# LSTM by cells: the first exact sweep becomes a second preparing sweep with short-fraction matmuls on 124 cells

## The reference

```python
x_proj = jnp.einsum('btd,gd->btg', x, W_ih) + b_ih + b_hh
def step(carry, xp):
    h, c = carry
    gates = xp + h @ W_hh.T
    i, f, g, o = jnp.split(gates, 4, axis=-1)
    c = jax.nn.sigmoid(f) * c + jax.nn.sigmoid(i) * jnp.tanh(g)
    h = jax.nn.sigmoid(o) * jnp.tanh(c)
    return ((h, c), h)
_, hs = jax.lax.scan(step, (h0, c0), jnp.swapaxes(x_proj, 0, 1))
```

## Time and profile before

| | us |
|---|---|
| median of the runs | 2495.29 |
| the profiled execution | 2494.4 |
| its span, first to last instruction | 2492.6 |
| busy TensorE matmul / weight load | 2193.6 / 1884.3 |
| busy VectorE / ScalarE / GpSimd | 1716.5 / 1504.2 / 156.2 |
| the three exact sweeps with their tests | 1664.4 to 2359.0 |

### The profile page before, as it was taken

One profiled execution on the slowest core, in us unless ns is written; L12 is line 12 of the kernel. 1 busy time (PEld: TensorE's weight loads), 2 busy tenths in 40 slices (PEclk: granted clock), 3 DMA queues, 4 the chain that ended last, 5 costly groups with the idle time before them and its releaser, 6 DMA issues.

```text
span 2492.6 us, 43835 instructions
## 1 busy us (share of the span) xinstructions
PE 2193.6 (88%) x13739; PEld 1884.3 (76%) x13739; DVE 1716.5 (69%) x3984; ACT 1504.2 (60%) x3023; POOL 156.2 (6%) x156
## 2 busy tenths in 40 slices
PE   4678989999999999999989899988888888888834
PEld 2457877888888888888878688878887888788723
DVE  5755878777777777777747777765655656555685
ACT  2344448888888878888843366655554555455515
POOL 2333000000000000000000000000000000000060
PEclk7789999999999999999999999999999999999975
DMA  3212320000000000000043122223332333233203
GB/s 93 80 63 82 94 95 20 28 22 28 26 25 25 28 27 25 25 29 24 22 123 93 36 99 112 104 108 113 114 114 84 114 115 107 90 115 115 74 2 101
DMA packets 94279, 174.11 MB, mean 70 GB/s; under 512 B 8088, under 2 KB 68500, under 8 KB 93858
## 3 DMA queue, kind: packets, MB, share of 16 engines
q1 hardware_dynamic: 62914, 86.59, 10.6%
q10 hardware_dynamic: 28108, 81.19, 10.4%
q0 software_dynamic: 3136, 4.76, 0.7%
HBM read 114.14 MB, written 58.36 MB: 69 GB/s over the span
## 4 chain that ended last, share of the span: by engine, by line
PE 52%; DVE 19%; ACT 8%; issue 8%; ACTq 2%; DMA 2%; DVEq 1%; POOL 0%; POOLq 0%
PE psum L600 23%; PE psum L595 11%; PE psum L746 8%; PE psum L703 4%; DVE scr L1542 3%; DVE scr L1540 3%; ACT scr L1012 2%; ACT scr L1020 2%; DMA out_dram<-wq 2%; DVE scr L1538 2%; DVE scr L1336 2%; DVE wp L1432 2%; DVE bufB L1460 1%; DVE bufB L1544 1%; ACTq L1031 1%
## 5 line engine op out<-in xcount | busy, mean ns | idle before, releaser
L920 ACT ACTIVATE counts<-psum 125x500 fp32r<-125x500 f32 (+1 forms) x663 | 719.9, 1121 | 158.3 <-PE psum L595 156.2
L600 PE MATMUL psum<-halves,counts 125*125 125x512 f32 x2500 | 741.9, 417 | 2.5 <-ACT counts L920 2.0
L1362 DVE TENSOR_TENSOR wx<-rs_buf 128x500 bf16<-128x500 bf16 (+2 forms) x1326 | 640.8, 530 | 130.3 <-PE psum L595 76.4
L746 PE MATMUL psum<-bufB,wx 128*128 x4800 | 602.6, 283 | 80.5 <-DVE bufB L1544 71.5
L746 PEld LDWEIGHTS psum<-bufB,wx 128*128 128x128 f32 x4800 | 564.1, 193 | 118.8 <-issue 108.0
L600 PEld LDWEIGHTS psum<-halves,counts 125*125 125x125 f32 x2500 | 416.9, 186 | 59.8 <-issue 4.5
L595 PE MATMUL psum<-wx 128*125 128x250 bf16 x2550 | 398.4, 276 | 5.3 <-DVE wx L1362 5.1
L595 PEld LDWEIGHTS psum<-wx 128*125 128x125 bf16 x2550 | 319.7, 138 | 91.1 <-DVE wx L1362 8.7
L1020 ACT ACTIVATE scr<-scr 128x125 f32<-128x125 f32 x300 | 92.2, 307 | 172.3 <-DVE scr L1542 172.3
L1544 DVE TENSOR_TENSOR bufB<-scr 128x125 f32 (+1 forms) x300 | 87.1, 290 | 146.6 <-ACT scr L1020 146.6
L703 PE MATMUL psum<-bufA,wx 128*128 (+1 forms) x800 | 180.1, 376 | 3.1 <-POOL rs_buf L457 3.1
(11 more groups left out here) (249 smaller groups left out, 2230.4 us busy)
## 6 DMA issues: line engine op xcount, KB each, us to landing
bufA<-gates_of_x ACTq DMA_DIRECT2D x144, 500.0 KB, 3.4
gates_of_x<-bufB SPq DMA_DIRECT2D x24, 1000.0 KB, 3.9
sums_by_feature<-scr SPq DMA_DIRECT2D x51, 125.0 KB, 2.1
x_times_eps_plus_sums<-rs_buf ACTq DMA_DIRECT2D x10, 625.0 KB
wx<-in_x_dram SPq DMA_DIRECT2D x25, 250.0 KB
x_plus_mix<-wx SPq DMA_DIRECT2D x25, 250.0 KB, 4.9
scr<-x_times_eps_plus_sums SPq DMA_DIRECT2D x50, 125.0 KB
x_times_eps_plus_sums<-scr SPq DMA_DIRECT2D x50, 125.0 KB
```

The costliest lines, as they stand in the source:

```text
L600: return mm(psum[0:TP, 3 + v, :], cnt[v][:, hi, :], xhl[:, hi, :, :].rearrange("p s d -> p (s d)"), start=(hi == 0), stop=(hi == NT - 1))
L746: return mm(gate_half(u, m, gate), whhv[:, k, (2 * gate + m) * P:(2 * gate + m + 1) * P], h, start=False, stop=(k == 1), skip_group_check= ...
L920: fn(cnt[v][:, :, 2 * GW * u:2 * GW * u + GW * g].rearrange("p h c -> p c h"), psum[0:TP, u % 3, 0:g * KEYS].rearrange("p (c h) -> p c h", ...
L1362: last = tt(to[:, 0:gs, :, :], tab2[:, 0:k, :].unsqueeze(1).broadcast_to([P, gs, k, 2]), keysT[v][:, part_, g0:g0 + gs, :].unsqueeze(2).br ...
```

## The change

The first of the exact sweeps is replaced by a second preparing sweep outside the loop. It has the same steps with the same gates, but another state buffer (`hs_r`, in the short-fraction format, 126 columns apart), other weights (`whr`, rounded to the same format, in the place of `wih`), and 124 of the 125 cells in its matmuls; the last cell's end is needed by nobody. Behind it stand three copies and no test. The counters of the loop start at 1. The gate slots in PSUM lie 126 columns apart instead of 125.

```diff
+        EV = CH + 1
+        w_near = bufB[:, 5000:5000 + 2 * G4].rearrange("p (k o) -> p k o", k=2)
+        w_rest = bufB[:, 5000 + 2 * G4:5000 + 3 * G4]
+        hs_r = xs_all[:, BIG - 100:BIG - 100 + (LS + 1) * 2 * EV].rearrange("p (t c j) -> p t c j", c=2, j=EV)
...
+        with nc.sbuf_tensor("rounded", [P, 2 * G4], F32R) as w_all:
+            pass
+        whr = w_all[:, :].rearrange("p (k o) -> p k o", k=2)
...
-            return psum[:, 4 * u + at, slot * CH:(slot + 1) * CH]
+            return psum[:, 4 * u + at, slot * (CH + 1):slot * (CH + 1) + CH]
...
+            pool.wait_ge(S["x1_v"], 2 * NB)
+            for c in range(2):
+                w, up, rest = whhv[:, c, :], w_near[:, c, :], w_rest[:, :]
+                pool.tensor_scalar(up, w, float(2 ** 12 + 1), None, ALU.mult).then_inc(S["near_q"], 1)
+                pool.wait_ge(S["near_q"], 3 * c + 1)
+                pool.tensor_tensor(rest, up, w, ALU.subtract).then_inc(S["near_q"], 1)
+                pool.wait_ge(S["near_q"], 3 * c + 2)
+                pool.tensor_tensor(up, up, rest, ALU.subtract).then_inc(S["near_q"], 1)
+            pool.wait_ge(S["near_q"], 6)
+            pool.wait_ge(S["pre_mm"], 4 * (LS // 2))
+            for c in range(2):
+                pool.tensor_copy(whr[:, c, :], w_near[:, c, :]).then_inc(S["w_low"], 1)
...
-            def time_step(done, t, u):
+            def time_step(done, t, u, w, state, cells):
 
-                h = [hs[:, ds(t, 1), c, :].rearrange("p t j -> p (t j)") for c in range(2)]
+                h = [state[:, ds(t, 1), c, 0:cells].rearrange("p t j -> p (t j)") for c in range(2)]
...
+            pe.wait_ge(S["w_low"], 4)
+            with pe.Fori(0, LS // 2) as i:
+                for u in range(2):
+                    time_step(2 * i + u, 2 * i + u, u, whr, hs_r, CH - 1)
+            pe.wait_ge(S["st_v"], 10)
 
             k_r_, go = pe.alloc_register("pe_sweeps"), pe.alloc_register("pe_go")
-            pe.reg_mov(k_r_, 0)
+            pe.reg_mov(k_r_, 1)
...
+            def sweep(base, before):
+
                 fetch(base, 0, 0)
+                if not isinstance(base, int):
+                    act.wait_ge(S["hth_act"], 2 * base)
                 fill(1, kept[1])
...
+            sweep(0, 0)
...
-            dve.memset(hs[:, 0, :, :], 0.0).then_inc(S["st_v"], 1)
+            dve.memset(hs_r[:, 0, :, :].bitcast(F32), 0.0).then_inc(S["st_v"], 1)
...
+            sweep(0, 0, hs_r)
+            dve.wait_ge(S["hh_v"], 2 + 2 * LS)
+            dve.tensor_copy(init_c[:, :, 1:CH], cN[:, :, 0:CH - 1]).then_inc(S["st_v"], 1)
+            dve.memset(hs[:, 0, :, 0:1], 0.0)
+            dve.tensor_copy(hs[:, 0, :, 1:CH], hs_r[:, LS, :, 0:CH - 1].bitcast(F32)).then_inc(S["st_v"], 1)
+            dve.wait_ge(S["st_v"], 9)
+            dve.tensor_copy(cN, init_c[:, :, :]).then_inc(S["st_v"], 1)
+            dve.wait_ge(S["st_v"], 10)
```

More of the change, by code:

```diff
@@ L1070, in _ @@
                 sweep_step(done, 1)
-                act.wait_ge(S["flag_v"], kv + 1)
+            sweep(0, 0)
+            k_r_, go = act.alloc_register("act_sweeps"), act.alloc_register("act_go")
+            act.reg_mov(k_r_, 1)
+            act.reg_mov(go, CH)
+            with act.While(lambda: act.snap(go) > act.snap(k_r_)):
+                kv = act.snap(k_r_)
+                sweep(act.snap(kv * LS), act.snap(kv * (LS // 2 - 1)))
+                act.wait_ge(S["flag_v"], kv)
                 act.reg_add(k_r_, kv, 1)
@@ L1383, in _ @@
                         dve.wait_ge(S[f"mix_st{v}"], 16 * ((NB + 1 - v) // 2))
-                    dve.memset(row_b[1], 0.0).then_inc(S["rz_v"], 1)
-                    dve.wait_ge(S["rz_v"], 1)
+                    dve.memset(row_b[1], 0.0).then_inc(S["zero_v"], 1)
+                    dve.wait_ge(S["zero_v"], 3)
                 hot(u, 0, u)
@@ L1532, in fill, with half_step @@
                 dve.tensor_copy(fill_to(u, 1), gates[0].rearrange("p g (m j) -> p m g j", m=2)).then_inc(S["fill_d"], 1)
-            def half_step(done, t, u, m):
+            def half_step(done, t, u, m, state):
                 n = 2 * done + m + 1
@@ L1543, in half_step, with sweep_step @@
                 dve.wait_ge(S["hth_act"], n)
[L1544 to L1548, removed]
+                tt(state[:, ds(t + 1, 1), m, 0:CH].rearrange("p t j -> p (t j)"), s_o[:, cut], th[:, cut], ALU.mult).then_inc(S["hh_v"], 1)
+            def sweep_step(done, t, u, state):
+                half_step(done, t, u, 0, state)
+                half_step(done, t, u, 1, state)
             kept = [[w[:, :, :] for w in pre_kept[v]] for v in range(2)]
@@ L1553, in _, with sweep @@
             dve.memset(psum[0:1, 6, 400:401], 0.0).then_inc(S["cnt_z"], 1)
[L1554 to L1560, removed]
+            cN = tg_c[0][:, 1, :].rearrange("p (c j) -> p c j", c=2)
+            def sweep(base, before, state):
                 fill(1, kept[1])
-                sweep_step(base, 0, 0)
+                sweep_step(base, 0, 0, state)
                 with dve.Fori(0, LS // 2 - 1) as i:
```

84 lines of the change are left out of this document (42 added, 42 removed).

## The result

The changed kernel takes 2490.83 us, the median of 11 runs (2484.08 to 2493.69), beside 2496.69 for the kernel before in the same session (11 runs, 2492.91 to 2501.01). The ratio is 0.9973, 95% interval 0.9963 to 0.9983: 5.9 us faster, where 13.7 were forecast. The profiled execution took 2492.4 us (before 2494.4), with a span of 2490.6 us and a mean granted clock of 0.906 (before 0.953).

What follows compares the result with a forecast made beforehand. The prediction took the chain of ScalarE and VectorE, more than busy TensorE, as the bound; 2.3 + 6.2 + 0.9 + 0.8 + 3.8 - 0.3 = 13.7 us off 2495.3 gave 2481.6, ends 2476.5 to 2493.2, stated range 2476 to 2491.

Steps and rivals of the forecast that it cites:

- Sweeps: Convergence tests of the loop: first test fails at about 9e-4, second passes at 1.1e-5, so two exact sweeps follow.
- rival 1: At the second test: it fails and three exact sweeps still run, +218.1 us, 2713.4; chance 0.12.
- rival 4: At the first test: it already passes, so one exact sweep is enough, 2249.8 us; chance 0.01.
- Start: New sweep's first matmul to first sigmoid: fewer instructions ahead of the sigmoid save 1.8 to 2.8 us, taken 2.3.
- 24 inner steps: New sweep's steps where TensorE ends last: the sigmoid starts sooner, 0.26 us each, 6.2 together (1.7 to 7.0).
- The clock: TensorE's granted clock in the new sweep, left open: gain 0.29 a step at 2.4 GHz, 0.07 to 0.29 at 1.2.
- 23 other steps: New sweep's steps ending on ScalarE: less register arithmetic ahead of the fill, 0.04 us each (0 to 0.1), 0.9 together.
- Last two steps: New sweep's end, where ScalarE idles 0.69 before the sigmoid: 0.2 to 0.4 us saved each, 0.8 together.
- Seam: Last half state's end to next sweep's sigmoid, 9.33 us today: 3.2 to 5.9 saved without the test, taken 3.8.
- Contention: GpSimd's splitting beside VectorE's products in the 16 bit sweep: costs 0 to 3 us, taken 0.3.
- rival 2: New sweep's matmuls: the short one is no faster at 124 columns, four passes, 0.21 apart; gain 7.4, 2487.9 us; chance 0.06.
- Rival 3: Only the test is saved, with TensorE at 1.2 GHz and the products delayed: gain 2.5, 2492.8 us; chance 0.03.

Runs made afterwards that it cites:

- e5_b16: Changed kernel with the second preparing sweep in 16 bit (8 significant bits), 125 cells, no splitting on GpSimd; one run, 2703.8 us, three exact sweeps.
- e2_warm: Changed kernel plus six full-format matmuls a step that nobody reads, in the second preparing sweep; 2485.70 us, ratio to before 0.9966.
- e13_slots126: Kernel before with the gate slots in PSUM 126 columns apart instead of 125, nothing else; one run, 2500.74 us beside 2500.54 of before.
- e14_full125: Changed kernel with its second preparing sweep in full format, without the splitting, gate slots 125 columns apart; one run, 2490.22 us beside 2500.54 of before.
- e1_nosplit: Changed kernel without GpSimd's six splitting operations; its two copies write the 32 bit weights straight into the short format; 2486.16 us, ratio to before 0.9960.
- e4_both: Changed kernel without the six splitting operations and with six added full-format matmuls a step in the new sweep; 2477.92 us, ratio to before 0.9928.
- e3_full: Changed kernel with the second preparing sweep in full format with the 32 bit weights and old state buffer, without the splitting; 2485.89 us, ratio to before 0.9968.
- e12_after8: Changed kernel with eight one-element ScalarE copies between the second preparing sweep and the loop of exact sweeps; one run, 2487.43 us.

## Why the forecast was wrong

The sign, the sweeps and the seam came out; the size did not, 5.9 for 13.7. That 2490.83 still lies inside the stated 2476 to 2491 is luck: 3.3 us of the gain come from the exact sweeps, for which the sum had no term.

- **Sweeps.** Two exact ones, 300 half states, 100 of them into the other buffer, 4000 matmul instructions, as predicted. The state's write into the short format left enough for the second test; rival 1 fell, and rival 4. That 8 bits are too few was borne out by e5_b16.
- **Start**, taken 2.3: 1.8, its lower end, the one for matmuls 0.23 apart.
- **24 inner steps, taken 0.26 each, 6.2: the step that failed.** They gave nothing, 4.38 us a step before and after. The range for 1.2 GHz went from 0.07 to 0.29 by whether the short matmuls come 0.10 or 0.23 apart, and I placed it by the 16 bit row as the nearer one. They come 0.21 apart at 0.50, exactly as one instruction of the full format does at that clock, and 0.11 at 1.00, again the same. The format halves the number of instructions, not what one takes, and at half the clock that is the old path again. Even the lower end was too high: behind a wait the two starts are 0.26 apart and the last matmul takes 0.42, so the path is 0.14 + 0.26 + 0.42 + 0.04 = 0.86 (1878.46 to 1879.32), where it was 0.88.
- **The clock.** "1.00 or 0.50" was left open and the gain taken nearly the same for both. That was the second half of the error. It stayed at 0.50 with 87% of the time busy, where the earlier trace rows has 1.00 with 89% before; e2_warm, which adds work back, got 1.00 and pairs of 8.44. The Trainium skill says that activity releases the throttle (TensorE: Matmul & The Clock Gate, What's actually happening); that more work brought the clock back agrees, though e2_warm worked 22.7 us without a pause first. The rival side of my own range should have had its weight. At 1.00 the 24 pairs would have given 0.4 each on top, more than the 0.29 that I saw as the limit, since the other step shortens too (4.33 for 4.48).
- **23 other steps**, taken 0.04 (bounds 0 and 0.1): 0.09, but not as I had it. I had these steps end on ScalarE. ScalarE's way to the fill did shrink, by 0.24 and so beyond my bound (0.96 us idle before, 0.72 in the new sweep, 0.88 in the exact sweeps of the changed kernel); that the constant base brings what lies below 0.88 fits, but no run takes it alone. At 0.50 TensorE then ends last here too and leaves 0.09 of it. The exact sweeps have a 0.09 of their own, which e13_slots126 and e14_full125 put down to the loops' structure. That is some 3.3 us in C and D that the sum did not have.
- **Last two steps**, taken 0.8: nothing, for the same reason. The sigmoid waits 0.61 and 0.77 there, 0.69 before.
- **Seam**, taken 3.8: 3.9. The first step there took 3.44, the clock at 0.50 for most of it and at 1.00 for its end.
- **Contention**, taken 0.3 (bounds 0 and 3): 3.1 in this kernel by e1_nosplit, 1.4 in two other pairs, and 0.4 at the copies. I placed the splitting before the recurrence's products, with 1.0 us for a GpSimd multiplication; it took 2.79, longer than a two-input one, so the six operations took 15.4 us instead of 11.4 and their last ones ran among the products. The Trainium skill's rule on shared interfaces (GPSIMD Engine Reference, Specifications) was the better guide than the row of one-input scalings: two-input products were the ones caught, though two of them and not all. TensorE never waited for the copies.

Sum of what was measured in the profiles: -1.8 (start) - 2.0 (steps, 0.6 of it the format) - 3.9 (seam) - 3.3 (exact sweeps) + 5.0 (A: 3.1 splitting, 1.5 late clock by chance in the first projections, 0.4 copies) = -6.0. Of the rivals, rival 2 was nearest by gain, 7.4, with the wrong cause: its spacing of 0.21 was for the full clock, where e2_warm has 0.11. Rival 3, TensorE at 1.2 GHz and the products delayed, had the right cause and 0.03; its 2.5 and the exact sweeps' 3.3 make 5.8.

## What to carry to other kernels

When a change takes work off TensorE, price its matmuls at both granted clocks, since the change may itself lower the clock; here half the instructions at half the clock left the step where it was. Filler matmuls into unread columns brought the clock back and with it the format's gain (e4_both, 18.0 us below before by its ratio, against 10.0 for e1_nosplit). Work given to an idle GpSimd is not free while VectorE runs two-input operations: schedule it by its measured length, or try first whether a plain copy into the format is good enough, as in e1_nosplit. And run the change of structure without the change of format before taking both: here e3_full alone gave the whole gain of the two.

## What the runs showed of the hardware

- The short-fraction matmul with 124 columns is one instruction: 0.21 us apart at a granted clock of 0.50 and 0.11 at 1.00, the same as each of the two instructions of the full format with 125 columns; the 16 bit one 0.10 at 0.50.
- GpSimd's multiplication of 128 x 1024 by a constant took 2.77 to 2.79 us, its two-input operation 2.35 to 2.41, its cast about 1.0.
- A two-input VectorE operation of 0.42 us that started just behind a two-input GpSimd operation ended 0.3 us after it: 2.37 to 2.54 us. Beside a GpSimd cast it took 0.93.
- In a sweep of full format matmuls the clock rose 3.8 to 5.7 us after the first one; with short ones and fillers it stayed at 0.50 for 10.7 to 22.7 us without a pause before it rose; with short ones alone it never did.
- A pause of TensorE of 2.86 us left the clock at 1.00 in the changed kernel; behind one of 2.85 at the same place it was at 0.50 for some 3 us in e12_after8.
- ScalarE's time ahead of a loop branch was 0.20 or 0.11 us for the same loop body, by the structure around it; the cause within that is open.
